# Two feed-forward stages joined into one loop over tile pairs in a graph layer on one core

## The reference

```
xn = layernorm(x)
# mix: a = xn + attention(...) @ wo + bo
x2 = (a - mean) * rsqrt(var + eps) * ln2_g + ln2_b
mix = a + relu(x2 @ w1 + b1) @ w2 + b2            # "feed-forward"
x  = x + gnn(xn) + mix
z  = layernorm(x)                                  # "quantised feed-forward"
q(v)  = clip(round(v * s), -128, 127) / s, s = 127 / max(|v| of the row, 1e-5)
tq(w) = clip(round(w / m), -1, 1) * m, m = mean |w|     # ternary weights
h  = silu(q(z) @ tq(w_gate).T) * (q(z) @ tq(w_up).T)
out = x + q(h) @ tq(w_down).T
```

## Time and profile before

| what | us |
|---|---|
| TensorE busy over the span | 1259.4 (88%) |
| VectorE, ScalarE, POOL busy | 786.4, 658.6, 364.2 |
| node stage, first to last product | 717.8 to 848.6 |
| projection, first to last product | 1036.6 to 1151 |
| feed-forward, first `z` to last product | 1159.2 to 1309.4 |
| a pair in its loop, relu to the same relu | 1246.82 to 1272.04 |
| quantised part, first `z` to last product | 1315.6 to 1424.4 |
| a tile in its loop, silu to silu | 1367.46, 1375.74, 1384.09, 1391.98, 1400.24 |
| last add on POOL ends, span ends | 1428.0, 1431.7 |

### The profile page before, as it was taken

How to read it: one execution, slowest core, us unless ns; L and a number is a source line. 1 busy time by engine, 2 the same in 40 slices (tenths; PEclk the granted TensorE clock), 3 DMA queues, 4 the chain that set the end, 5 groups by cost and what they waited for, 6 DMA issues and landing times. The chain is left out here.

```text
span 1431.7 us, 19932 instructions
## 1 busy us (share of the span) xinstructions
PE 1259.4 (88%) x6953; PEld 1091.9 (76%) x6953; DVE 786.4 (55%) x1198; ACT 658.6 (46%) x960; POOL 364.2 (25%) x213
## 2 busy tenths in 40 slices
PE   7989989999999999997597975999599948996785
PEld 4556789999999999997486855999577747885453
DVE  7879445555555565655523765665242227543584
ACT  7275345545555555555534212333254432434574
POOL 1300022324141332222101111535122229320023
PEclk9999999999999999999698986999899979998799
DMA  7001400202012020201455434232343325100022
GB/s 193 18 18 30 98 1 1 62 0 62 19 42 62 0 62 0 62 0 63 123 157 153 141 131 152 76 112 67 103 144 87 85 80 183 43 1 1 5 67 72
DMA packets 71418, 99.30 MB, mean 69 GB/s; under 512 B 27241, under 2 KB 52165, under 8 KB 70863
## 3 DMA queue, kind: packets, MB, share of 16 engines
q1 hardware_dynamic: 66956, 82.96, 20.4%
q0 software_dynamic: 4416, 15.73, 3.5%
HBM read 77.04 MB, written 21.63 MB: 69 GB/s over the span
## 5 line engine op out<-in xcount | busy, mean ns | idle before, releaser
L1053 POOL TENSOR_TENSOR cos_sin_lo<-cos_sin,cos_sin_hi 125x1024 fp32r<-125x1024 f32 (+1 forms) x40 | 95.7, 2394 | 349.2 <-ACT cos_sin_hi L1127 349.2
L1114 ACT ACTIVATE cos_sin<-part_turn 125x512 f32<-125x512 f32 (+1 forms) x80 | 50.1, 627 | 148.7 <-DVE part_turn L1242 148.7
L451 PE MATMUL p_cnt<-hot_s,hot_d 125*125 125x418 bf16 x540 | 113.7, 362 | 1.8 <-DVE hot_d L384 1.8
L668 PE MATMUL p_h<-x 128*125 128x512 f32 x400 | 110.2, 404 | 0.0
L880 PE MATMUL p_o<-h_hi,a_lo 125*125 125x342 f32 x300 | 97.1, 324 | 11.4 <-POOL a_lo L772 11.4
L382 DVE TENSOR_SCALAR hot_s<-iota_h,ends 125x1250 bf16<-125x1250 f16 x180 | 97.5, 541 | 16.1 <-PE p_cnt L451 14.1
L1327 PE MATMUL p_w<-x,mix_hi_v 128*128 128x416 f32 (+1 forms) x384 | 105.1, 355 | 0.0
L1327 PE MATMUL p_w<-x,mix_hi_k 128*128 128x416 f32 (+1 forms) x384 | 104.2, 352 | 0.0
L1327 PE MATMUL p_w<-x,mix_hi_q 128*128 128x416 f32 (+1 forms) x384 | 104.2, 352 | 0.0
L451 PEld LDWEIGHTS p_cnt<-hot_s,hot_d 125*125 125x125 bf16 x540 | 63.5, 140 | 51.6 <-DVE hot_d L384 40.7
L880 PE MATMUL p_o<-h_hi,a_hi 125*125 125x342 f32 x300 | 96.7, 322 | 0.0
(11 more groups left out here) (295 smaller groups left out, 3268.7 us busy)
## 6 DMA issues: line engine op xcount, KB each, us to landing
x_in<-in_x_dram SPq DMA_DIRECT2D x30, 448.0 KB
attn_dram<-attn_t SPq DMA_DIRECT2D x8, 625.0 KB, 3.9
at_in<-attn_dram SPq DMA_DIRECT2D x10, 500.0 KB, 4.5
x_rows<-in_x_dram SPq DMA_DIRECT2D x10, 448.0 KB
gnn_dram<-gnn SPq DMA_DIRECT2D x10, 448.0 KB
x_in<-gnn_dram SPq DMA_DIRECT2D x10, 448.0 KB
out_dram<-result SPq DMA_DIRECT2D x10, 448.0 KB
mix_in_v<-in_L_mix_wv_dram SPq DMA_DIRECT2D x8, 512.0 KB, 6.3
```

Source lines behind the costliest of these rows:

```text
L451: last = pe.matmul(p_cnt[0:T, t % 2, n, 0:w], hot_d[:, j, 0:T], hot_s[:, j, a:a + w], start=False, stop=False)
L668: last = pe.matmul(p_h[0:T, i % 2, n, :], left[i % 2][:, k, :], right[:, k, cols], start=(k == 0 and m == 0), stop=(k == K8 - 1 and m == 2))
L1053: pool.tensor_tensor(full(cs_lo, k), full(cs, k), f32(full(cs_hi, k)), ALU.subtract).then_inc(s_cslo[0], 1)
L1114: act.activation(step_view(cs, k, 1), rows(part, k), ACT.Sin, scale=TWO_PI)
```

## The change

1. Node stage: four magnitude pieces behind each of tiles 1 to 3; the ternary pieces three behind each of tiles 5 to 8; each is transposed there by TensorE, kept by ScalarE and stored already turned.
2. Projection: the row sum comes from the add's accumulator; the inverse root of each tile is made on POOL by a power and one Newton step; w1 is scaled by the norm's scale while it is split; the norm's shift times w1 is added to b1 (32 products of one column).
3. The two last stages become one block without hardware loops, in which the quantised work of pair c−1 and c−2 is written between the feed-forward work of pair c. The affine step on VectorE and the clips are gone (the fp32 add of the lift is the only step), the result is scaled and added on VectorE from PSUM, POOL's last add is gone.

```diff
@@ node_features
-    FIRST = 4
+    MAGNITUDES_AT = {1: range(0, 4), 2: range(4, 8), 3: range(8, 12)}
+    TERNARY_AT = {5: range(0, 3), 6: range(3, 6), 7: range(6, 9), 8: range(9, 12)}
...
             for n in range(PIECES):
+                if n + 2 < PIECES:
+                    pool.wait_ge(s_tern, 2 * n + 2)
+                    load_piece(PIECES + n + 2)
                 store_piece(n)                # now waits for s_wk, the kept turned piece
...
+            def keep_turned(n):               # ScalarE, behind keep_h_hi
+                act.wait_ge(s_wt, n + 1)
...
+                act.activation(turned[:, n % 2, :]..., p_wt[:], ACT.Copy).then_inc(s_wk, 1)
...
+            def turn(n):                      # TensorE, behind products(i)
+                pe.wait_ge(s_tern, 2 * n + 2)
+                pe.wait_ge(s_wk, n)
+                for b in range(8):
...
+                    last = pe.transpose(p_wt[:, b, :], ternary[...], core.ident_b[:])
@@ project_attention
+            for f in range(F4):
+                for k in range(K8):
+                    last = pe.matmul(p_c[:, f:f + 1], w1_raw(k)[:, f * 128:(f + 1) * 128], b2c[:, k:k + 1], start=(k == 0),
+                                     stop=(k == K8 - 1))
...
+            dve.wait_ge(s_c, 1)
+            dve.tensor_tensor(core.c1[:], p_c[:], b1c, ALU.add).then_inc(s_ck, 1)
+            for i in range(2, NT):
+                attention_lo(i)
+                add(i - 1)
@@ row_rstd, on POOL: six small steps per tile
+    pool.tensor_scalar(var, core.var[:, col], 1.0 / D, LN_EPS, ALU.mult, ALU.add).then_inc(s_step, 1)
+    pool.tensor_tensor(rough, var, core.minus_half[:, col], ALU.pow).then_inc(s_step, 1)
...
@@ feed_forward_and_quantised, ScalarE
+            def keep_zt(i):
+                act.wait_ge(s_t, i + 1)
+                act.wait_ge(s_1, F4 * (i // 2))
...
+            for c in range(CH + 2):           # each line only where its tile exists
+                silu(2 * c - 3)
+                round_hidden(2 * c - 4)
+                normalise(2 * c + 2)
+                hidden(c, 0)
+                keep_hidden(2 * c - 4)
+                round_x(2 * c - 2)
+                normalise8(2 * c - 1)
+                round_hidden(2 * c - 3)
+                hidden(c, 1)
+                normalise(2 * c + 3)
+                keep_hidden(2 * c - 3)
+                keep_zt(2 * c + 2)
+                round_x(2 * c - 1)
+                hidden(c, 2)
+                hidden(c, 3)
+                keep_zt(2 * c + 3)
+                keep_x(2 * c - 2)
+                squares(2 * c)
+                keep_x(2 * c - 1)
+                squares(2 * c + 1)
+                normalise8(2 * c)
+                silu(2 * c - 2)
@@ VectorE
+            for c in range(CH + 2):
+                hidden8(2 * c - 3)            # product, maximum, scale and lift
+                scale_x(2 * c - 2)            # maximum, scale and lift
+                hidden_halves(c, 0)
+                hidden_halves(c, 1)
+                result(2 * c - 4)
+                scale_x(2 * c - 1)
+                keep_zt(2 * c + 2)
+                hidden_halves(c, 2)
+                result(2 * c - 3)
+                hidden_halves(c, 3)
+                keep_zt(2 * c + 3)
+                add(2 * c)
+                add(2 * c + 1)
+                hidden8(2 * c - 2)
@@ TensorE
+            for c in range(CH + 2):
+                hidden(c, 0)
+                transpose_hidden(2 * c - 4)
+                hidden(c, 1)
+                down(2 * c - 4)
+                transpose_hidden(2 * c - 3)
+                transpose_z(2 * c + 2)
+                hidden(c, 2)
+                down(2 * c - 3)
+                hidden(c, 3)
+                transpose_z(2 * c + 3)        # waits for VectorE's keep_zt(2c+2)
+                outer(2 * c)                  # w2; waits for the halves of all four
+                transpose_x(2 * c - 2)
+                outer(2 * c + 1)
+                transpose_x(2 * c - 1)
+                gate_up(2 * c - 2)
+                gate_up(2 * c - 1)
@@ POOL
+            for c in range(CH):
+                residual(2 * c + 2)           # two adds of 1024 columns, the second behind normalise
+                residual(2 * c + 3)
+                row_rstd of tiles 2c and 2c + 1, each behind its squares
```

More of the change, by code:

```diff
@@ L1458, in _ @@
             pair(PAIRS - 1, False)
[L1461 to L1469, removed]
-    act.mul(neg_mean, sums, -1.0 / D).then_inc(s_stat, 1)
-    act.wait_ge(s_stat, count + 2)
-    act.activation(junk, rows_in, ACT.Square, bias=neg_mean, accum_out=squares).then_inc(s_stat, 1)
 def project_attention(core):
@@ L1950, in quantised_forward @@
[L1950 to L1959 removed]
+        gate = sb("gate", [T, FF])
+        hid8 = sb("hidden8", [T, FF])
@@ L2092, in _ @@
[L2092 to L2102 removed]
+                if i >= 2:
+                    act.wait_ge(s_d, i - 1)
+                act.activation(ht[:, i % 2], p_q[i % 2][:, 0:F4, 0:T], ACT.Copy).then_inc(s_hk, 1)
@@ L2173, in _, with result @@
-            tile(NT - 2, 0, more=False)
-            tile(NT - 1, 1, more=False)
+                row_scale(i, hid8[:], most2, s_m2, (2,))
+                dve.tensor_scalar(hid8[:], hid8[:], most2[:, 2:3], MAGIC, ALU.mult, ALU.add).then_inc(s_lift2, 1)
+            def result(i):
+                dve.wait_ge(s_d, i + 1)
+                row = rows[:, i, :].rearrange("p (b n) -> p b n", b=2)
+                dve.scalar_tensor_tensor(row, p_a[0:T, i % 2], factor[:, i, 2:3], row, ALU.mult, ALU.add).then_inc(s_out, 1)
@@ L2176, in _ @@
         @block.tensor
         def _(pe):
-            pe.wait_ge(s_ib, 1)
-            def transpose_weights(first, past):
-                for n in range(first, past):
-                    if n >= 2:
-                        pe.wait_ge(s_wk[n % 2], n // 2)
-                    blocks, _, _ = rounds(n)
-                    for b, at in enumerate(blocks):
-                        last = pe.transpose(p_tr[:, n % 2, b, :], core.ternary[:, n // 4, at:at + 128], ident_b[:])
-                    last.then_inc(s_wt, 1)
@@ new lines, in outer @@
+            def outer(i):
+                pe.wait_ge(s_hlo, F4 * (i // 2 + 1))
+                if i == 0:
+                    pe.wait_ge(s_wlo, F4)
+                if i in (2, 3):
+                    pe.wait_ge(s_y, i - 1)
+                if i >= 4:
+                    pe.wait_ge(s_out, i - 3)
+                tile = slice((i % 2) * T, (i % 2 + 1) * T)
+                for n in range(2):
+                    for f in range(F4):
+                        for m, (left, right) in enumerate(((hid_lo, w2_hi), (hid_hi, w2_lo), (hid_hi, w2_hi))):
+                            last = pe.matmul(p_a[0:T, i % 2, n, :], left[:, f, tile], right[:, f, n * 512:(n + 1) * 512],
+                                             start=(f == 0 and m == 0), stop=(f == F4 - 1 and m == 2))
+                last.then_inc(s_2, 1)
```

918 lines of the change are left out of this document (377 added, 541 removed).

## The result

The kernel after took 1442.97 us (median of 7 runs, 1437.97 to 1444.55) against 1430.92 before (7 runs): ratio 1.0077, 95% interval [1.0055, 1.0099], 12 us slower. The forecast was 1423. The profiled execution took 1442.33 us with a span of 1440.5. Cut at the same places as before, the span went up by 8.8 us; that this is less than 12 comes from the profiled execution of before, which lay 2.6 us above its median.

The account below looks back on a forecast made before the run. TensorE was taken as the busy engine nearly everywhere. Joined stage −20.5, node stage +3 and projection +9.5 summed to −8.0 us, put on the median: 1423 us, range 1404 to 1442.

Parts of the forecast that it names:

- gap 1: Joined stage, each full pair: TensorE waits 4.5 us for the odd tile's rounded hidden rows, 2.7 of it from POOL's adds.
- pair 1: Joined stage, the pair without down products and without gap 1: forecast to take 37.1 us.
- I add about 1.1 per gap: Joined stage: slow clock after each TensorE gap costs about 1.1 us, between 0 and 1.7.
- +2 for some slow clock: Projection, one-column products: 2 us for slow clock within their 10.4 us.
- the 1.5 of the node stage: Node stage: some slow clock after the groups of transposes costs 1.5 us.
- Rival A: Interleaved loop and turns: slow clock costs 3.4 us per gap instead of 1.1, +18, turns +5; 1446 us; chance 0.17.
- My sign for it: Joined stage: a clock of the loop under 0.85 would show Rival A.
- Gap 2: Joined stage, each full pair: TensorE waits 4.6 us between the last hidden product and W2's, besides a 0.9 us transpose.
- Work per pair: Joined stage: TensorE's own work in a full pair is 36.1 us.
- my low end: Projection: the one-column products cost only 3 us, as 32 steps of 0.05.
- Rival D: Joined stage: square and silu need two table loads per pair, 1.3 us each; +2 to +8, 1428 us; chance 0.08.
- Rival C: Joined stage: gap 1 at most 1.75 us, the wait before W2 about 3, no slow stretches; 1405 us; chance 0.12.

Follow-up runs that it names:

- filled_gaps: Kernel after with matmuls without use put into two of TensorE's waits in each of pairs 2 and 3; 1435.18 us, ratio 1.0035.
- late_adds: full_order with POOL's residual adds of the next pair held back until this pair's hidden halves are made; 1405.76 us, ratio 0.9813.
- columns_last: Kernel after with the 32 one-column products moved behind the last tile of the projection; 1436.56 us, ratio 1.0034.
- full_order: Kernel after with reordered work around W2 and the odd tile's hidden rows rounded and copied before x work on ScalarE; 1415.36 us, ratio 0.9901.
- no_residual_adds: Kernel after without POOL's two residual adds per tile, semaphores still counted up; 1425.92 us, ratio 0.9956.

## Why the prediction was wrong
The sum was 20 us too low. In the profiled executions 17 of them show (forecast −8.0, measured +8.8 us of span); the other 3 are that the profiled execution of before lay 2.6 above its median and that of after 0.6 below. Of the 17, 13.5 fell on the joined stage, 3.5 on the node stage and 2.0 on the projection, and the stretches in front gave 2 back. The structure of the sum held. Its term for the slow clock failed, and in the joined stage two waits: gap 1, and one in pair 1.

*The slow clock.* The step that failed is "I add about 1.1 per gap", and with it the "+2 for some slow clock" of the projection and the 1.5 of the node stage. I read it from two gaps: 4.4 us with a slow stretch, 1.9 without. Here two waits of 1.66 and 1.21 us around a turn of 0.6 were followed by a slow stretch, and the half clock lasted 6.8 us at each gap of pair 2, not 3.4.
- By my own terms a full pair is 51.9 us (mean); less 36.1 of work and waits of 5.4, 1.45 and 4.0, 4.9 is left for the clock, not 2.2. Half of the time that TensorE is recorded busy in the two slow windows gives the same, 5.0, and filled_gaps gave back 4.2 and 3.8 per pair.
- In the node stage 3.4 + 3.4 + 6.8 us were at half clock (the last from 846.2); one of the four groups of turns left none. TensorE is recorded busy for 12.0 of these 13.6 us, so about 6 are lost instead of 1.5.
- In the projection TensorE is recorded busy for 12.3 of the 7.2 + 6.5 us: about 6.2 lost instead of 2.

Excess: 5.4, 4.5 and 4.2, about 14 us. The waits below add 8.5 more, and the remaining terms together gave about 6 back.

*Rival A* had this mechanism, with 3.4 per gap, and gave 1446; the time came out 3 below it. That it came so near is partly luck: a slow stretch of 6.8 us cost 2.2 to 2.8 us, since TensorE stands still in part of it, not every gap left one (pair 4 none), and longer waits made up the rest. My sign for it, a clock of the loop under 0.85, did not show either: it was 0.87 in pairs 2 and 3. Its argument against, that the quantised loop with waits of about 1 us stays at 0.92, was no evidence for gaps of 4 to 6. filled_gaps shows the mechanism.

*Gap 1.* Forecast 4.5; measured 5.7 and 5.2, by the mechanism named: placed behind the x rounding, the hidden lift at 2.47. I gave 2.7 to the adds; the small factor of one column per row, 1.90 instead of 0.16, was missing, and no row of before had shown it. Missed altogether was the 1.45 us behind it: the transposes of `z` share their PSUM banks with the hidden ones and wait for ScalarE's copy of these (`s_hk`). Together 2.4 us per full pair more than forecast.

*Pair 1* had 37.1 and took 41.0: a wait of 3.7 us between its third and fourth hidden product, for a relu queued behind the x rounding. I had placed no such wait there, and without POOL's adds it is gone.

*Gap 2.* 4.0 in two parts (2.4 and 1.6) against 4.6, by the mechanism named: right. The profile names no releaser for the first part, but it ends as VectorE's split of `z` does (1291.8).

*Work per pair.* 36.1 forecast, 36.3 measured in late_adds: right. The start took 33.65 against 33.3, pair 4 37.4 against 38, the end 35.75 against 36.0: right. Pair 0's W2 took 14.0 against 12.8.

*Node stage.* A group of turns took 4.8 (forecast 4.7), the end has 5.2 without TensorE instead of 13.4 (8 less), and nothing waits at the magnitudes: right. Not seen was that a stage without turns would be only 9 us faster, since the third piece's load then holds VectorE, and through it TensorE.

*Projection.* The 64 records would be 6.8 at full clock by the 0.107 step (forecast 6.7; the step of 0.05 behind my low end stands in no row), and the wait was 1.4 (1.7). With 6.2 of clock that is 14.4, and the stage rose by 11.5, so 2.9 came back instead of 0.9. Of that 1.65 shows between the last product and `z` (6.55 instead of 8.2). About 1.4 more was no merit of the change: over the first 10 us of the stage, with TensorE busy throughout, the clock was 0.85 instead of 0.71.

*Rival D* is off: one table load of 1283 ns stands in the joined stage (ahead of the first silu), with squares and relus on both sides of later silus. By the reading of the Trainium skill that rival D took (ScalarE: Activation LUTs, "Table sets: the hidden batching unit") a second load per pair was due; the trace has none, so the measurement decides for the other reading. *Rival C* gave 1405, and late_adds measured 1405.76, but that is chance: C had pairs of 41 us, and in late_adds they are 37.0, in another order, with the node stage and the projection costing more than C assumed.

The Trainium skill (SBUF — State Buffer, "Who interferes with whom") also says that VectorE with two SBUF inputs contends with POOL's reads. That part I left out; the factor of one column has two such inputs, and its 1.90 us beside the adds and 0.16 without them agree with it. The result add from PSUM stayed at 1.28 and the row maximum at 1.21, as the same section says.

## What to carry to other kernels
When stages are interleaved by hand, follow each chain through each engine's queue to its last link; moving one link only hands the wait on, and the same gain may be had by moving another engine's work from beside the chain. Price TensorE's waits together with the half clock that follows: in the full pairs here 10.9 us of waits brought 4 to 5 us of it. Place small work one instruction at a time where a large one already covers it, and ask what the other engines and the loads do in that place: three pieces in a row on VectorE, the third behind its load, made TensorE wait even with the turns they fed left out. And compare a rival with the result part by part: two here met a measured time partly or wholly by luck.

## What the runs showed of the hardware
- One-column fp32 products, recorded back to back, saw the granted clock fall from 1.00 to 0.50 (kernel after, at 1068.0, for 13.7 us; columns_last, between 1155.8 and 1160.3); without them the same stretch was at 1.00.
- An instruction of VectorE on one column, with two SBUF inputs, took up to 1.93 us instead of 0.16 beside an add of 2.4 us on POOL; a cast of 0.29 took up to 2.48 (full_order). Without POOL's adds (no_residual_adds) the same cast took 0.29 at most.
- Waits of 5.7, 1.45, 2.4 and 1.6 us in a pair came with two stretches of 6.8 us at half clock; with the longest and the 2.4 filled by other products there was none (filled_gaps).
- With all small products in place and waits of at most 1.9 us per place, the loop ran at 1.00 throughout (full_order, pairs 2 and 3).
